# Four-layer network on one core: the join of the last two layers written in another order

## Chip, cores and metric

One Trainium2 chip, one of its cores. The metric is the device time of one execution in microseconds (us). Engines are named as in the profile: PE is TensorE, DVE is VectorE, ACT is ScalarE, POOL is GpSimd, SP is SyncE, whose queue here only issues transfers.

## What is computed

Four layers in a row, each `x = x + ffn(cond(x))`, on 4 sequences of 256 tokens with 256 features. The condition of a layer is a gain per token and feature (it depends on `side` and `cond`, not on x) times `sigmoid(x)`. The change lies between the last step of the third layer's feed-forward part and the first attention head of the fourth layer:

```python
# third layer, behind gate and up: RMS norm, a quantisation, the down product
h = rms_norm(h, ln_weight)
return bit_linear(h, w_down)          # rounds h per token to 8 bits, times ternary weights
...
# fourth layer
x = x + ao                            # ao: attention of 16 heads, each of 128
h = rmsnorm(x, ln1_w)
q = (h @ wq).reshape(b, s, H, HD)
k = (h @ wk).reshape(b, s, H, HD)
v = (h @ wv).reshape(b, s, H, HD)
scores = jnp.einsum('bqhd,bkhd->bhqk', q, k) / np.sqrt(HD)
attn = jax.nn.softmax(jnp.where(causal, scores, -1e9), axis=-1)
```

## The kernel before, in words

Every engine has its own list of instructions, written out by hand, and the lists meet at semaphores. T is 1,024 tokens, P is 128, W is 512; features lie on the partitions, in KD = 2 blocks, so that x consists of NCH = 4 chunks of 128 x 512. ORDER takes the two chunks of the first 512 tokens (n = 0, 1) ahead of those of the last 512 (n = 2, 3). A float32 product is made of three passes: a value is split in a high part (rounded to fp32r) and a low part (the rest), and the passes are high x high, low x high, high x low.

**The tail of layer 2 (the third layer).** The last four of eight tiles of 128 tokens, u = 4 to 7, go through this chain: `rounds(u)` on VectorE (L1551 H, then L1555 HQ, both 128x1024), `turn_hidden(u)` on TensorE (eight transposes, L1630), `product_turned(u)` on ScalarE (HT, L1461), `product(u)` on TensorE (L1641), `out(u)` on ScalarE (OT, L1468), `back(u)` on TensorE (two transposes, L1649). Behind back(7) lies the result of the last 512 tokens, which `residual(2)` and `residual(3)` (L2369) add to x.

**The head of layer 3 (the fourth layer).** For each half n of the tokens: `sigmoid` on ScalarE (L293), `with_gain` on VectorE (four pieces of 128x256 a half, L324, which give XC), then the norm: `squares` on ScalarE (L1709), `add_up` on TensorE (sums over the features, L1717), `means` on VectorE (L1724), `roots` on ScalarE (L1730, Sqrt), `factors` on VectorE (L1735), `spread_out` on TensorE (the factors to all partitions, L1741), `normalise` on VectorE (HN, L1750), `high` on ScalarE (XH, L1759), `low` on VectorE (XL, L1766).

**The weights.** A group g of two heads has 2,048 columns in RAW, four parts of 512 (GCOL). ScalarE makes the high part WH of each (L2244), GpSimd the low part WL (L2211, `split_low`). Group 0 is split by GpSimd in one go ahead of everything else of layer 3. The transfer of group 1 is issued when all four chunks of XC are there.

**Attention in halves.** `project(i, c)` makes one of six blocks of q, k and v of half i (c = 0, 1, 4, 5: six passes of 128x512, L2566; c = 2, 3: twelve of 128x256, L2561), into bank c % 2, which ScalarE (even c) or VectorE (odd c) empties (L2251, L2363). Half 0 is group 0 with the first 512 tokens, half 1 group 0 with the last 512. The steps of a half stand in a table, PLANS: S is scores (TensorE L2637, L2638; the row maximum on VectorE L2449; the exponential on ScalarE L2302), N divides by the sum (VectorE L2457, L2462), T turns (TensorE L2645, ScalarE L2309), A is attention times V (TensorE L2655, L2656), O the output product, D c the block c of the next half's projection, H a part of a later group's weights (ScalarE, then GpSimd). B occurs in PLANS[0] alone: spread_out, normalise, high and low of the second half of the tokens. All engines walk the same table, each doing its own share of a step. Before the first projection of a half 0 or 1 TensorE waits for the XL of its tokens:

```python
if c == 0 and half == 0:

    pe.wait_ge(w_low, 4 * g + 3)
if c == 0 and i < 2:

    pe.wait_ge(norm.xl, 2 * (i + 1))
```

Below stand the functions that the diff touches.

Of the kernel before, what the change touches and what calls it, by code (L numbers as in the profile page):

```python
# [1781 lines left out]
PLANS = {0: "S0 S1 B0 N0 H0 S2 H1 T0 N1 S3 D0 H2 T1 N2 D1 N3 D2 A0 T2 A1 T3 D3 A2 D4 A3 D5 H3".split(),  # L1782
# [30 lines left out]
def all_steps():  # L1813

    return [("C", n, 0) for n in range(6)] + [step for i in range(NHALF) for step in steps_of(i)]
# [264 lines left out]
def layer3(nc, k, io, ahead):  # L2080
# [3 lines left out]
    with ExitStack() as ctx:  # L2084
# [122 lines left out]
        def split_low(pool, g, m):  # L2207

            pool.wait_ge(w_high, 4 * g + m + 1)
            c = slice(m * GCOL, (m + 1) * GCOL)  # L2210
            pool.tensor_tensor(WL[g % 2][:, c], RAW[g % 2][:, c], WH[g % 2][:, c].bitcast(F32),  # L2211
                               ALU.subtract).then_inc(w_low, 1)

        @block.gpsimd
        def _(pool):
            ahead_gpsimd(pool)
            for m in range(4):
                split_low(pool, 0, m)

            pool.wait_ge(cond.xc, 2)  # L2220
            pool.memset(MASK[:], 0.0).then_inc(mask, 1)
            pool.wait_ge(mask, 1)

            pool.affine_select(out=MASK[:], in_=MASK[:], compare_op=ALU.is_ge, fill=NEG,
                               base=P, pattern=[[-1, 2 * P]], channel_multiplier=1).then_inc(mask, 1)
            for kind, n, at in all_steps():
                if kind == "H":
                    split_low(pool, at, n)
                    if (n, at) == (0, 1):
                        pool.memset(ex.TW[:, 0], 1.0).then_inc(ex.tw_one, 1)  # L2230
                if kind == "E":
                    ex.split_low(pool, at, n)
            ex.gpsimd(pool)
# [13 lines left out]
        def _(act):  # L2247

            def evacuated(i, c):
                if c % 2 == 0:  # L2250
                    evacuate(act, i, c, lambda out, in_: act.activation(out, in_, ACT.Copy))  # L2251
# [17 lines left out]
            product_turned(5)  # L2269
            out(4)  # L2270
            act.wait_ge(cond.xc, 2)
            norm.squares(act, 0)
            product_turned(6)
            out(5)
            product_turned(7)
            out(6)
            norm.roots(act, 0)
            out(7)
            norm.high(act, 0)
# [8 lines left out]
            evacuated(0, 4)  # L2288
            for kind, n, at in all_steps()[6:]:
# [33 lines left out]
                if kind == "B":  # L2323
                    norm.high(act, 1)
# [33 lines left out]
        def _(v):  # L2358
# [12 lines left out]
            def with_gain(n):  # L2371
                v.wait_ge(cond.sig, n + 1)
                v.wait_ge(k.g_done, LAYERS * NCH)
                conditioned(v, k, cond, 1, n)
# [4 lines left out]
            rounds(5)  # L2379
            with_gain(0)  # L2380
            with_gain(1)
            rounds(6)
            rounds(7)
            norm.means(v, 0)
            norm.factors(v, 0)
            v.wait_ge(ln_in, 16)
            norm.normalise(v, 0)
            norm.low(v, 0)
            residual(2)
            residual(3)  # L2390
            evacuated(0, 1)
            with_gain(2)
            with_gain(3)
            evacuated(0, 3)
            norm.means(v, 1)
            norm.factors(v, 1)
            evacuated(0, 5)
# [40 lines left out]
            for kind, n, at in all_steps()[6:]:  # L2438
# [38 lines left out]
                if kind == "B":  # L2477
                    norm.normalise(v, 1)
                    norm.low(v, 1)
# [43 lines left out]
        def _(pe):  # L2523
# [79 lines left out]
            turn_hidden(4)  # L2603
            turn_hidden(5)
            product(4)
# [3 lines left out]
            norm.add_up(pe, 0)  # L2609
# [5 lines left out]
            norm.spread_out(pe, 0)  # L2615
# [4 lines left out]
            for c in range(4, 6):  # L2620
                project(0, c)
            for kind, n, at in all_steps()[6:]:
# [40 lines left out]
                if kind == "B":  # L2663
                    norm.spread_out(pe, 1)
# [130 lines left out]
```

## Time and profile before

| | |
|---|---|
| median of 3 runs | 899.87 us (897.52, 899.87, 900.35) |
| profiled execution, its own time | 899.28 us |
| its span, first to last instruction | 897.6 us |
| TensorE busy (matmul) | 759.3 us, 85% |
| VectorE busy | 577.1 us, 64% |
| ScalarE busy | 437.8 us, 49% |
| GpSimd busy | 240.5 us, 27% |
| mean granted clock of TensorE | 0.931 |

The span is the time between the first and the last instruction; the execution's own time is 1.7 us longer. Busy shares are averages over four layers with different limits, so they do not tell what a change at one place is worth. The join lies between about 337 and 396 us of the span. The granted clock is a share of full speed: 1.00 is 2.4 GHz, 0.50 is 1.2 GHz. In the timeline a row gives the start, the duration, the engine, the line and the operation; in square brackets stands how long the engine had been idle before it and who released it. Where several like instructions are merged, the duration is that of all of them.

### The profile page before, as it was taken

What the parts mean: (1) busy time and instruction counts of PE and PEld (TensorE: products, weight loads), DVE (VectorE), ACT (ScalarE), POOL (GpSimd) and SP (SyncE); (2) the same over time, 40 slices, a digit from 0 to 9 for tenths busy, and PEclk for the clock granted to TensorE, in tenths of its full rate; (3) what the DMA queues carried; (4) which work ended last, traced back from release to release, by engine and by line L of the source; (5) the groups of instructions that cost most, each with busy time, mean ns of one, the idle gap of its engine ahead of it and who ended that gap; (6) DMA issues with size and microseconds to landing.
All of it is one profiled execution on the core that took longest, in us unless ns stands there. A gap on an engine that the chain in (4) does not pass through costs nothing.

```text
span 897.6 us, 11277 instructions
## 1 busy us (share of the span) xinstructions
PE 759.3 (85%) x3633; PEld 576.1 (64%) x3633; DVE 577.1 (64%) x1285; ACT 437.8 (49%) x878; POOL 240.5 (27%) x245
## 2 busy tenths in 40 slices
PE   1886785978785555799999999999969999999997
PEld 0433453634453134688888988888857888888885
DVE  5998889879988896556566566755664233232233
ACT  5895452235414646456455555654654334334342
POOL 5310112320140623011021021201111455555553
PEclk9999897789896878899999999999997999999998
DMA  4000003923222000210110101101010632323421
GB/s 149 2 1 1 0 0 111 381 66 106 82 71 70 1 0 1 94 48 1 48 39 11 47 1 48 37 1 37 1 38 11 154 95 59 95 46 73 93 55 47
DMA packets 37422, 49.84 MB, mean 56 GB/s; under 512 B 18574, under 2 KB 29942, under 8 KB 35702
## 3 DMA queue, kind: packets, MB, share of 16 engines
q1 hardware_dynamic: 36310, 46.90, 17.1%
q0 software_dynamic: 768, 2.10, 0.7%
q8 instruction: 30, 0.49, 0.2%
q10 hardware_dynamic: 288, 0.14, 0.1%
q14 instruction: 26, 0.21, 0.1%
HBM read 42.99 MB, written 6.13 MB: 55 GB/s over the span
## 4 chain that ended last, share of the span: by engine, by line
PE 59%; DVE 7%; ACT 2%; issue 1%; POOL 1%; DVEq 0%; ACTq 0%
PE bank L2000 15%; PE bank L2566 10%; PE bank L2016 8%; PE bank L2580 5%; PE bank L2561 5%; PE bank L2655 3%; PE bank L2638 3%; PE bank L2645 2%; PE bank L2656 2%; PE bank L2637 1%; PE bank L1614 1%; PE bank L1717 1%; DVE H L1551 1%; DVE XC L324 1%; DVE H L1530 1%
## 5 line engine op out<-in xcount | busy, mean ns | idle before, releaser
L2044 DVE TENSOR_TENSOR B_l<-bank,TW_l 128x512 f32<-128x512 f32 (+1 forms) x50 | 34.5, 691 | 134.3 <-PE bank L2000 131.3
L2211 POOL TENSOR_TENSOR WL<-RAW,WH 128x512 fp32r<-128x512 f32 x32 | 41.8, 1312 | 232.4 <-ACT WH L2244 232.4
L2069 POOL TENSOR_TENSOR HL_l<-H_l,HH_l 128x512 fp32r<-128x512 f32 (+1 forms) x50 | 64.9, 1298 | 121.9 <-ACT HH_l L2061 121.9
L2302 ACT ACTIVATE EX<-EX,nm 128x128 f32<-128x128 f32 (+1 forms) x128 | 57.0, 446 | 72.6 <-DVE nm L2453 72.6
L2053 ACT ACTIVATE S_l<-bank 128x512 f32<-128x512 f32 (+1 forms) x50 | 29.9, 599 | 86.1 <-PE bank L2000 85.9
L159 POOL TENSOR_TENSOR WV<-EUK,V 128x512 f32<-128x512 f32 x16 | 23.8, 1495 | 152.6 <-DVE GAIN L274 89.9
L2467 DVE TENSOR_TENSOR AL<-bank,AH 128x256 fp32r<-128x256 f32 x64 | 27.2, 424 | 56.6 <-ACT AH L2316 56.6
L2566 PE MATMUL bank<-XH,WH 128*128 128x512 f32 x128 | 60.3, 471 | 3.7 <-DVE XL L1766 2.8
L2000 PE MATMUL bank<-XH,WH 128*128 128x512 f32 (+1 forms) x136 | 55.0, 405 | 0.0
L2000 PE MATMUL bank<-XL,WH 128*128 128x512 f32 (+1 forms) x136 | 54.5, 401 | 0.0
L2000 PE MATMUL bank<-XH,WL 128*128 128x512 f32 (+1 forms) x136 | 54.5, 401 | 0.0
L2566 PE MATMUL bank<-XH,WL 128*128 128x512 f32 x128 | 51.9, 406 | 0.0
L2566 PE MATMUL bank<-XL,WH 128*128 128x512 f32 x128 | 51.7, 404 | 0.0
L2061 ACT ACTIVATE HH_l<-H_l 128x512 fp32r<-128x512 f32 (+1 forms) x50 | 31.5, 631 | 36.5 <-PE bank L2016 29.7
L2449 DVE CUSTOM_DVE_ANT_0 EX<-bank,MASK 128x128 f32<-128x128 f32 (+1 forms) x128 | 40.7, 355 | 13.1 <-PE bank L2638 12.5
L1983 POOL TENSOR_TENSOR WL<-RAW,WH 128x512 fp32r<-128x512 f32 x27 | 35.0, 1296 | 44.9 <-ACT WH L1976 44.9
L506 ACT ACTIVATE MARK<-SC,THR 128x1536 bf16<-128x1536 bf16 (+1 forms) x30 | 43.0, 1509 | 6.2 <-PE bank L727 6.2
L2462 DVE TENSOR_SCALAR PN<-EX,rr 128x128 f32<-128x128 f32 (+1 forms) x128 | 38.9, 353 | 2.5 <-PE bank L2645 0.2
L2655 PE MATMUL bank<-PT,V 128*128 128x256 f32 x128 | 38.4, 381 | 2.4 <-ACT PT L2309 2.4
L2638 PE MATMUL bank<-K,Q 128*128 128x256 f32 x128 | 38.7, 384 | 0.0
L2561 PE MATMUL bank<-WH,XH 128*128 128x256 f32 x128 | 38.5, 301 | 0.0
L2316 ACT ACTIVATE AH<-bank 128x256 fp32r<-128x256 f32 x64 | 24.6, 384 | 27.7 <-PE bank L2656 26.2
(319 smaller groups left out, 2198.5 us busy)
## 6 DMA issues: line engine op xcount, KB each, us to landing
RAW<-l_attn SPq DMA_DIRECT2D x8, 1024.0 KB, 4.8
WE<-l_experts SPq DMA_DIRECT2D x1, 6144.0 KB, 22.8
TW_l<-routed SPq DMA_DIRECT2D x14, 256.0 KB, 4.2
RAW<-l_w SPq DMA_DIRECT2D x3, 1024.0 KB
RAW<-l_experts SPq DMA_DIRECT2D x6, 512.0 KB, 3.9
TW_l<-routed SPq DMA_DIRECT2D x14, 192.0 KB, 3.3
sorted_x<-ZERO SPq DMA_DIRECT2D x1, 1920.0 KB, 8.0
XIN<-sorted_x SPq DMA_DIRECT2D x15, 128.0 KB, 2.2
```

Of the source, the lines that this page charges most:

```text
L506: act.activation(MARK[:, n % RING, 0:cols], SC[:, at:at + cols], ACT.Sign, bias=THR[:, i:i + 1]).then_inc(mark, 1)
L2000: mm = pe.matmul(self.k.banks[2 * ((q + 1) % 2) + o][0:rows], w[i % self.SLOTS][:, at:at + rows], x[:, h, n * W:(n + 1) * W], start=(s == ...
L2016: mm = pe.matmul(self.k.banks[4 + 2 * m + n][:], w[i % self.SLOTS][0:rows, at:at + P], x[0:rows, q % 4], start=((i, f, s) == (0, 0, 0)), s ...
L2069: pool.tensor_tensor(self.HL[0:rows, q % 4], self.H[0:rows, q % 2], self.HH[0:rows, q % 4].bitcast(F32), ALU.subtract).then_inc(self.h_low, 1)
L2211: pool.tensor_tensor(WL[g % 2][:, c], RAW[g % 2][:, c], WH[g % 2][:, c].bitcast(F32), ALU.subtract).then_inc(w_low, 1)
L2302: act.activation(EX[:, s, a:b], EX[:, s, a:b], ACT.Exp, bias=nm[:, s, i:i + 1], scale=scale, accum_out=rs[:, s, i:i + 1]).then_inc(expd, 1)
L2449: v.tensor_tensor_reduce(EX[:, s, a:b], banks[2 + s][:, a:b], MASK[:, 2 * P - (b - a):], 1.0, NEG, ALU.add, ALU.max, accum_out=mx[:, s, i: ...
L2561: mm = pe.matmul(out[:, a * 2 * HD:(a + 1) * 2 * HD], x[:, h, t * P:(t + 1) * P], w[slot][:, at:at + 2 * HD], start=(p == 0), stop=(p == l ...
L2566: mm = pe.matmul(out[:], w[slot][:, at:at + HD], x[:, h, half * W:(half + 1) * W], start=(p == 0), stop=(p == len(passes) - 1))
L2580: mm = pe.matmul(banks[m][:], w[g % 2][:, at:at + P], x[:, head, here(i)], start=(head == 0 and p == 0), stop=(head == 1 and p == 2))
L2638: pe.matmul(out[:, P:3 * P], Q[:, n // 2, c + P:c + SEQ], K[:, n // 2, c:c + SEQ], start=True, stop=True).then_inc(scores, 1)
L2655: pe.matmul(out[:, 0:SEQ], V[:, t, d], PT[:, s, 0:SEQ], start=True, stop=False)
```

## The change

Four things are written in another order; no arithmetic is added or taken away.

- `split_low` of group 0: GpSimd's four instructions become four of VectorE, put between its other steps. GpSimd waits for them (`w_low` at 4) before it goes on with the later groups.
- The first half's norm moves ahead in the tail of layer 2: with_gain(0) and (1) stand ahead of rounds(5), means and factors ahead of rounds(7), add_up behind product(4), spread_out behind turn_hidden(5).
- "Conditions other half ahead of first keys": with_gain(2) and (3) stand ahead of the evacuation of the first key block, `evacuated(0, 1)`.
- The second half's factors go between projections: spread_out(1) between project(0, 4) and project(0, 5), normalise and high right behind; low becomes the step K0 at the head of PLANS[0], B0 is gone, and in the table the first projections of half 1 (D0, D1) stand ahead.

```diff
-PLANS = {0: "S0 S1 B0 N0 H0 S2 H1 T0 N1 S3 D0 H2 T1 N2 D1 N3 D2 A0 T2 A1 T3 D3 A2 D4 A3 D5 H3".split(),
+PLANS = {0: "K0 S0 S1 D0 H0 N0 S2 H1 T0 N1 D1 T1 S3 N2 D2 A0 H2 T2 N3 D3 A1 T3 A2 D4 A3 D5 H3".split(),
...
         @block.gpsimd
         def _(pool):
             ahead_gpsimd(pool)
-            for m in range(4):
-                split_low(pool, 0, m)
...
+            pool.wait_ge(w_low, 4)
             for kind, n, at in all_steps():
...
         @block.scalar
...
             product_turned(4)
-            product_turned(5)
-            out(4)
             act.wait_ge(cond.xc, 2)
             norm.squares(act, 0)
+            out(4)
+            norm.roots(act, 0)
+            product_turned(5)
             product_turned(6)
             out(5)
+            norm.high(act, 0)
             product_turned(7)
             out(6)
-            norm.roots(act, 0)
             out(7)
-            norm.high(act, 0)
...
             norm.roots(act, 1)
             evacuated(0, 4)
+            norm.high(act, 1)
...
-                if kind == "B":
-                    norm.high(act, 1)
...
         @block.vector
...
             residual(0)
             residual(1)
             rounds(4)
-            rounds(5)
+            split_low(v, 0, 0)
             with_gain(0)
             with_gain(1)
+            rounds(5)
             rounds(6)
+            norm.means(v, 0)
+            split_low(v, 0, 1)
+            norm.factors(v, 0)
             rounds(7)
-            norm.means(v, 0)
-            norm.factors(v, 0)
             v.wait_ge(ln_in, 16)
             norm.normalise(v, 0)
+            split_low(v, 0, 2)
             norm.low(v, 0)
+            split_low(v, 0, 3)
             residual(2)
             residual(3)
-            evacuated(0, 1)
             with_gain(2)
             with_gain(3)
+            evacuated(0, 1)
             evacuated(0, 3)
             norm.means(v, 1)
             norm.factors(v, 1)
+            norm.normalise(v, 1)
             evacuated(0, 5)
...
-                if kind == "B":
-                    norm.normalise(v, 1)
+                if kind == "K" and at == 0:
                     norm.low(v, 1)
...
         @block.tensor
...
             turn_hidden(4)
+            product(4)
+            norm.add_up(pe, 0)
             turn_hidden(5)
-            product(4)
+            norm.spread_out(pe, 0)
             turn_hidden(6)
             product(5)
             back(4)
-            norm.add_up(pe, 0)
             turn_hidden(7)
             product(6)
             back(5)
             product(7)
             back(6)
-            norm.spread_out(pe, 0)
             back(7)
             for c in range(4):
                 project(0, c)
             norm.add_up(pe, 1)
-            for c in range(4, 6):
-                project(0, c)
+            project(0, 4)
+            norm.spread_out(pe, 1)
+            project(0, 5)
...
-                if kind == "B":
-                    norm.spread_out(pe, 1)
```

TensorE in the tail of layer 2, before, from the sums of the first half (L1717) to the spreading of its factors (L1741); L1630 are transposes of HQ, L1641 products, L1649 transposes back:

```order
L1717 MATMUL bank4<-ONES,SQ3 128x1 x8
L1630 MATMUL bank1<-IDB,HQ2 128x128 x8
L1641 MATMUL bank2<-WT2,HT2 128x256 x8
L1649 MATMUL bank5<-IDF,OT2 128x128
L1649 MATMUL bank7<-IDF,OT2 128x128
L1641 MATMUL bank3<-WT2,HT2 128x256 x8
L1649 MATMUL bank5<-IDF,OT2 128x128
L1649 MATMUL bank7<-IDF,OT2 128x128
L1741 MATMUL bank6<-IDF,rstd3 128x128 x4
```

The same place in the change, from product(4) on:

```order
L1641 MATMUL bank2<-WT2,HT2 128x256 x8
L1717 MATMUL bank4<-ONES,SQ3 128x1 x8
L1630 MATMUL bank1<-IDB,HQ2 128x128 x8
L1741 MATMUL bank6<-IDF,rstd3 128x128 x4
L1630 MATMUL bank0<-IDB,HQ2 128x128 x8
L1641 MATMUL bank3<-WT2,HT2 128x256 x8
L1649 MATMUL bank5<-IDF,OT2 128x128
```

The sums now stand behind the first of four products, and the factors behind one set of transposes more; three products and three sets of transposes back, which stood ahead of the factors, now stand behind them.

VectorE from the first half's means (L1724) on, before:

```order
L1724 TENSOR_SCALAR ms3<-bank4 128x4
L1735 RECIPROCAL rstd3<-rt3 128x4
L1750 SCALAR_TENSOR_TENSOR HN3<-XC,LN3,bank6 128x512 x2
L1766 TENSOR_TENSOR XL3<-HN3,XH3 128x512 x2
L2369 TENSOR_TENSOR X<-X,bank5 128x512
L2369 TENSOR_TENSOR X<-X,bank7 128x512
L2363 COPY K3<-bank1 128x512
```

and in the change, where L2211 is `split_low`, L1551 and L1555 are rounds(7), and L2368 is the residual:

```order
L1724 TENSOR_SCALAR ms3<-bank4 128x4
L2211 TENSOR_TENSOR WL3_0<-RAW3_0,WH3_0 128x512
L1735 RECIPROCAL rstd3<-rt3 128x4
L1551 TENSOR_SCALAR H2<-H2,s2_2 128x1024
L1555 TENSOR_SCALAR HQ2<-H2 128x1024
L1750 SCALAR_TENSOR_TENSOR HN3<-XC,LN3,bank6 128x512 x2
L2211 TENSOR_TENSOR WL3_0<-RAW3_0,WH3_0 128x512
L1766 TENSOR_TENSOR XL3<-HN3,XH3 128x512 x2
L2211 TENSOR_TENSOR WL3_0<-RAW3_0,WH3_0 128x512
L2368 TENSOR_TENSOR X<-X,bank5 128x512
```

Three of the four low parts of the weights stand between the steps of the norm, and rounds(7) stands behind the factors (L1735) where it stood ahead of the means.

TensorE at the start of PLANS[0], before: scores of steps 0 and 1, the second half's factors (L1741), scores of step 2, the first turn (L2645), scores of step 3, then the first projection of half 1 (L2566):

```order
L2637 MATMUL bank2<-K3,Q3 128x128
L2638 MATMUL bank2<-K3,Q3 128x256
L2637 MATMUL bank3<-K3,Q3 128x128
L2638 MATMUL bank3<-K3,Q3 128x256
L1741 MATMUL bank7<-IDF,rstd3 128x128 x4
L2637 MATMUL bank2<-K3,Q3 128x128
L2638 MATMUL bank2<-K3,Q3 128x256
L2645 MATMUL bank4<-IDF,PN3 128x128 x3
L2637 MATMUL bank3<-K3,Q3 128x128
L2638 MATMUL bank3<-K3,Q3 128x256
L2566 MATMUL bank0<-XH3,WH3_0 128x512
```

and in the change (its line numbers are 3 or 4 higher), from the end of the first scores on:

```order
L2642 MATMUL bank2<-K3,Q3 128x256
L2641 MATMUL bank3<-K3,Q3 128x128
L2642 MATMUL bank3<-K3,Q3 128x256
L2569 MATMUL bank0<-XH3,WH3_0 128x512
L2569 MATMUL bank0<-XL3,WH3_0 128x512
L2569 MATMUL bank0<-XH3,WL3_0 128x512
L2569 MATMUL bank0<-XH3,WH3_0 128x512
L2569 MATMUL bank0<-XL3,WH3_0 128x512
L2569 MATMUL bank0<-XH3,WL3_0 128x512
L2641 MATMUL bank2<-K3,Q3 128x128
L2642 MATMUL bank2<-K3,Q3 128x256
L2649 MATMUL bank4<-IDF,PN3 128x128 x3
```

The first projection of half 1 (six passes) stands ahead of the scores of step 2 and of the first turn, and the factors are no longer in between.

## Rows read from the trace of the kernel before

**Rows 1.** The page, first part: busy us, share of the span and count by engine

```profile
PE 759.3 (85%) x3633; PEld 576.1 (64%) x3633; DVE 577.1 (64%) x1285; ACT 437.8 (49%) x878; POOL 240.5 (27%) x245
```

**Rows 2.** By stretch: length, busy PE, PEld, DVE, ACT, POOL, clock, DMA share, GB/s

```profile
357.00:358.00 1.00, 0.00 (x0) 0.00 (x0) 0.96 (x2) 0.97 (x2) 0.00 (x0) 0.94 0.00 0
...
395.70:651.00 255.30, 254.39 (x1497) 224.46 (x1496) 162.07 (x590) 141.06 (x416) 35.68 (x28) 1.00 0.09 28
```

**Rows 3.** The chain that ended last, in order of time: start, us, what

```profile
359.02 5.47 PE bank L2566 x12
...
382.70 2.56 PE bank L2566 x6
385.26 0.35 PE bank L2645 x3
385.61 1.39 PE bank L2566 x6
```

**Rows 4.** Timeline of TensorE: start, us, engine, line, operation, idle before and releaser

```profile
342.31 1.04 PE L1630 MATMUL bank<-IDB,HQ 128*128 128x128 bf16 x8 [4.88 <-DVE HQ L1555]
...
345.54 1.92 PE L1641 MATMUL bank<-WT,HT 128*128 128x256 bf16 x8
...
349.30 1.84 PE L1717 MATMUL bank<-ONES,SQ 128*128 128x1 f32 x16
...
352.73 1.05 PE L1641 MATMUL bank<-WT,HT 128*128 128x256 bf16 x8
...
354.82 1.16 PE L1741 MATMUL bank<-IDF,rstd 128*128 128x128 f32 x8 [0.82 <-DVE rstd L1735]
...
359.02 0.77 PE L2566 MATMUL bank<-XH,WH 128*128 128x512 f32 x1 [2.83 <-DVE XL L1766]
...
368.03 1.95 PE L1717 MATMUL bank<-ONES,SQ 128*128 128x1 f32 x16 [0.66 <-ACT SQ L1709]
...
380.52 0.90 PE L2645 MATMUL bank<-IDF,PN 128*128 128x128 f32 x3 [4.82 <-DVE PN L2462]
```

**Rows 5.** Timeline of VectorE

```profile
338.74 1.84 DVE L1551 TENSOR_SCALAR H<-H,s 128x1024 f32<-128x1024 f32 x1
...
344.57 1.66 DVE L324 SCALAR_TENSOR_TENSOR XC<-SG_l,GF,GAIN 128x256 f32<-128x256 f32 x4
346.15 0.75 DVE L1551 TENSOR_SCALAR H<-H,s 128x1024 f32<-128x1024 f32 x1
...
354.59 0.18 DVE L1735 RECIPROCAL rstd<-rt 128x4 f32<-128x4 f32 x1 [3.25 <-ACT rt L1730]
...
357.53 1.35 DVE L1766 TENSOR_TENSOR XL<-HN,XH 128x512 fp32r<-128x512 f32 x2
...
378.35 2.12 DVE L2462 TENSOR_SCALAR PN<-EX,rr 128x128 f32<-128x128 f32 x2
...
381.56 0.55 DVE L2462 TENSOR_SCALAR PN<-EX,rr 128x128 f32<-128x128 f32 x2
```

**Rows 6.** Timeline of GpSimd

```profile
337.53 5.85 POOL L2211 TENSOR_TENSOR WL<-RAW,WH 128x512 fp32r<-128x512 f32 x4 [7.71 <-ACT WH L2244]
...
378.04 1.32 POOL L2211 TENSOR_TENSOR WL<-RAW,WH 128x512 fp32r<-128x512 f32 x1 [30.09 <-ACT WH L2244]
```

**Rows 7.** Timeline of ScalarE

```profile
340.32 1.15 ACT L293 ACTIVATE SG_l<-X 128x512 f32<-128x512 f32 x2
...
351.65 1.02 ACT L1461 ACTIVATE HT<-bank 128x1024 bf16<-128x1024 bf16 x1 [1.37 <-PE bank L1630]
...
353.06 1.28 ACT L1730 ACT_TABLE_LOAD   x1
354.35 0.20 ACT L1730 ACTIVATE rt<-ms 128x4 f32<-128x4 f32 x1
...
356.87 1.29 ACT L1759 ACTIVATE XH<-HN 128x512 fp32r<-128x512 f32 x2 [1.95 <-DVE HN L1750]
```

**Rows 8.** Transfers into the tile RAW, 366 to 380 us: time from issue to landing

```profile
DMA to landing us min/median/max: 4.7/6.4/8.0
```

More of the change, by code:

```diff
@@ L2205, in _, with split_low @@
             sp.wait_ge(stored, 16 * NCH)
-        def split_low(pool, g, m):
-            pool.wait_ge(w_high, 4 * g + m + 1)
+        def split_low(eng, g, m):
+            eng.wait_ge(w_high, 4 * g + m + 1)
             c = slice(m * GCOL, (m + 1) * GCOL)
-            pool.tensor_tensor(WL[g % 2][:, c], RAW[g % 2][:, c], WH[g % 2][:, c].bitcast(F32),
+            eng.tensor_tensor(WL[g % 2][:, c], RAW[g % 2][:, c], WH[g % 2][:, c].bitcast(F32),
                                ALU.subtract).then_inc(w_low, 1)
```

## Prediction

> **What bounds the kernel now.** I read the page first: TensorE is busy 85% of the span, every other engine much less [rows 1]. That average says nothing about the join, so I took busy time by stretch. From 395.7 to 651 us TensorE works 254.39 of 255.30 us at a granted clock of 1.00 (2.4 GHz) [rows 2]: once attention is in its stride TensorE alone sets the end, and every microsecond by which half 1 begins earlier reaches the end of the program. Half 1 begins at 395.7. Then I read the timelines of the four engines between 337 and 396 us for what TensorE waits for:
>
> - 4.88 us ahead of the transposes at 342.31, until VectorE has written HQ [rows 4];
> - 2.83 us ahead of the first projection at 359.02, until XL is there [rows 4];
> - 0.66 us ahead of the second half's sums at 368.03, for the squares [rows 4];
> - 4.82 us ahead of the first turn at 380.52, for PN [rows 4].
>
> Two waits cost more than their length. In the stretch from 357 to 358 us the granted clock leaves 1.00, with TensorE without work [rows 2], and the twelve matmuls of the first two projections then take 5.47 us; six take 1.39 us at full clock [rows 3]. The same shows behind the wait for PN: 2.56 us for six at 382.70, against 1.39 for the next six [rows 3].
>
> **The change part by part.** I followed each engine's new list by hand with the durations of the rows.
>
> *VectorE up to the gains.* GpSimd's four low parts lie from 337.53 to 343.4 [rows 6], and beside them an H of 1,024 columns takes 1.84 us, where it takes 0.75 alone [rows 5]. The change takes GpSimd's work away from here. H and HQ of tile 4 then take about 1.4 us (338.74 to 340.15) and one low part on VectorE 0.63: it has shape and types of XL, whose pair takes 1.35, and starts are 0.63 apart [rows 5]. That is a near match, so its bounds are close: 0.6 to 0.7. The first sigmoid is ready at about 340.9 [rows 7], and the four pieces of gain take 1.6 us [rows 5]: XC is there at 342.5 instead of 346.2.
>
> *The factors.* The transposes of tile 4 start at 340.2 instead of 342.31, HT at 341.5 behind the sigmoids, product(4) at 342.4 with 1.92 us as at half clock [rows 4]. ScalarE makes the squares meanwhile. The sums take 1.8 us [rows 4] behind product(4), to 346.0. Mean 0.17, root 0.2, one low part 0.63 and reciprocal 0.18: factors at 346.9 instead of 354.8 [rows 5]. The Sqrt table load of 1.28 us [rows 7] falls between 344.6 and 345.9, while TensorE adds up, and costs nothing; were the sums 1.3 us faster it would be what is waited for.
>
> *Start of the projections.* The factors are spread by 348.2. HN takes 1.4 to 349.7, then come a low part, XH of two chunks (1.29 us for the pair [rows 7]) and XL by 352.0. TensorE is not ready for it: behind the spreading stand two sets of transposes, three products (0.87 us to the next start at full clock, 1.05 each in the row [rows 4]) and the transposes back. HT of tile 7 waits on ScalarE behind the two XH until 351.2 and takes 0.95 to its end [rows 7], product(7) 352.2, OT 0.42, and the last transposes end at 353.8. The first projection starts there: **5.2 us earlier** than 359.02. What is late next is thus the tail of layer 2, not the norm; XL, and with it the three low parts put ahead, has 1.8 us in hand.
>
> *Clock at the first projections.* Ahead of it TensorE now has gaps of 0.9 and 0.3 us where it had 0.82 and 2.83. Two projections at full clock take 2.8 instead of 5.47 [rows 3]: **2.6 us**. Bounds: 0 if the clock is at 1.2 GHz again, 2.7 if not.
>
> *Conditions ahead of the first keys.* Between 353.9 and 357.0 VectorE does residual(2), (3) and the gains, the squares are ready at 358.2, and the sums of the second half are due behind projection 3 at 359.3. The wait goes: **0.7 us** [rows 4]. The key block is emptied at 357.6 and its bank is wanted at 358.0; if the cover of 0.3 us is gone, it costs what the gains are late. The transfer of group 1's weights is issued with the gains, at 357 instead of 367, lands at most 8.0 us later [rows 8], at 365, and ScalarE wants it at 369.9: nothing.
>
> *Factors between the projections, and the plan.* Spreading (0.9 us) only changes place. The new wait there would be for the reciprocal: sums end at 361.0, the root is at 361.5, projection 4 covers until 362.4. After projection 5 (364.7) VectorE empties a bank and makes XL (1.9 us) while TensorE does two scores (1.3): a wait of 0.7 for half 1's first projection. Then the row maxima (0.8), the exponential (0.9) and N (0.75) against projection 6 and the scores (2.0): a wait of 0.5 at the first turn. The old wait of 4.8 us had room for HN, XL and N in a row; now HN is made under projection 5. And GpSimd's low parts of group 1 now run beside N of steps 1 to 3. One such meeting stands in the rows: a pair of PN takes 2.12 us beside a low part of 1.32, and 0.55 without [rows 5, 6]. Following the starts, two of the three meet it for a part, 0.7 to 0.8 us at TensorE. Sum: 4.8 - 0.7 - 0.5 - 0.8 = **2.8 us**. Bounds: 4.8 if nothing is waited for, 0 if the chain is as long as before.
>
> *Clock behind it.* At 380.52 the turn takes 0.90 against 0.35, the projection 2.56 against 1.39, and the scores between them 0.9 against 0.65 [rows 3, 4]: **2.0 us**, all of which hangs on there being no wait of several microseconds.
>
> *Nothing* for GpSimd (it waits for work there), for SP and for the new wait of GpSimd for the four low parts, done at 352.6, 18 us ahead of its next.
>
> Sum: 5.2 + 2.6 + 0.7 + 2.8 + 2.0 = 13.3. The profiled execution took 899.28 us, so 886.0; the median of the runs is 0.6 above it: **886.6 us**.
>
> *Two rules weighed.* The table load takes 1.28 us and the activation behind it starts 0.01 us after its end [rows 7]. The Trainium skill ("ScalarE: Activation LUTs", What ACT_TABLE_LOAD costs) adds a drain of about 1.38 us to each switch. By that rule the root and all behind it would come 1.1 us later and the sum would be 12.2 instead of 13.3; the row is of the same instruction, so I keep 13.3.
>
> The meeting of PN with a low part costs between 0.7 and 0.8 us by the starts [rows 5, 6]. The Trainium skill ("SBUF — State Buffer", Who interferes with whom) says that the one of VectorE and GpSimd that comes second is held for the whole of the other's instruction. By that rule, if all three meetings fell worst, the loss would be three times 1.3 us instead of 0.8, and the sum 10.2; the trace agrees that the loser waits (1.57 us lost in the pair above) but the starts that I follow are not the worst.
>
> **The rivals.**
>
> *A: low clock at the first projections.* The gaps of 0.9 and 0.3 us and a partly idle stretch before 346 suffice to keep or bring 1.2 GHz. For it: it fell after a wait of 2.83 us only [rows 2, 4]. Against it: until 354 it stood with gaps of like size. Time: 886.6 + 2.6 = 889.2.
>
> *B: the stall at the first turn comes back.* The exponential needs its table (1.28) behind XH, N needs VectorE behind XL and the maxima, and GpSimd holds PN. If that is as long as before, 2.8 and 2.0 us are not gained: 891.4.
>
> *C, slower than before: TensorE stays at 1.2 GHz through the whole stretch.* The change replaces long waits by short ones; if these keep the clock low from 341 until half 1 begins, the first two projections cost 2.6 us more, the ten others 2.56 - 1.39 = 1.17 each, so 11.7, and turns, scores and products with V some 3.5 (0.9 of it stands in the term for the clock above). Time: 886.6 + 17.8 = 904.4, slower by 0.5%. It decides from 13.3 us on, about ten projections at half clock. Against it: in this trace continuous projections brought the clock back each time, after the 5.47 us for twelve matmuls and ahead of the 1.39 at 385.61 [rows 3], and the stretch is mostly such work.
>
> *D: no change.* The trace has no other limit ahead of 395.7 that could swallow 13 us, and the listing shows the steps moved as described, so this is left with the smallest chance.
>
> **How the numbers follow.** Forecast 0.66, A 0.16, B 0.12, C 0.02, D 0.02, and 0.02 for A and B together (894). The range: below, all new waits (2.0 us) vanish and the run lies 1.1 low, as 897.52 to 900.35 scatter by 1.4 about their middle: 883.5. Above it takes in A and B: 891.5. About 0.3% (2.7 us) is what a measurement of this kernel can tell from no change. Faster by more than that, under 897.2: forecast, A, B and both, 0.96; within: 0.02; slower: 0.02.
>
> **What would show it.** Right: no GpSimd work from 330 to about 370 us except the mask; H near 0.78 us each; factors near 347; the first projection at 353 to 355 behind the last transposes back, not behind XL; its two first blocks in 2.8 us; no wait over 1 us at the first turn; half 1 at 381 to 383; from there to the end the same length as before. Wrong: a first projection released by XL, a wait for PN over 2 us, six matmuls of 2.5 us behind 354, or a tail from half 1 on that is longer than 502 us.

## The result, and the profile after

The changed kernel takes 887.58 us (median of 4 runs, 886.44 to 892.8) against 899.99 us before: a ratio of 0.9877, 95% interval 0.9853 to 0.9902. Forecast were 886.6 us and a range of 883.5 to 891.5. The profiled execution took 887.66 us with a span of 885.9; before, 899.28 and 897.6. So the size came out within 1 us, but the two largest of the five terms of the sum behind it did not, and part of the agreement is luck; the section on the prediction says which part.

The page, first part, of the changed kernel, as [rows 1]:

```profile
span 885.9 us, 11278 instructions
PE 758.4 (86%) x3633; PEld 573.6 (65%) x3633; DVE 576.8 (65%) x1289; ACT 437.6 (49%) x878; POOL 234.4 (26%) x241
```

TensorE runs the same number of instructions, and its busy time over the whole program is the same to 0.9 us. The join, the stretch in which the change acts, tells more: TensorE is busy there for 42.6 of 58.2 us before and for 40.5 of 49.0 now, so 7.0 of the 9.1 us that went are waiting and 2.1 are busy time, which hangs on the clock. Timeline of TensorE in the tail of layer 2 and at the first projections (as [rows 4]):

```profile
341.06 0.62 PE L1630 MATMUL bank<-IDB,HQ 128*128 128x128 bf16 x8 [2.84 <-DVE HQ L1555]
343.23 1.89 PE L1641 MATMUL bank<-WT,HT 128*128 128x256 bf16 x8 [1.54 <-ACT HT L1461]
344.91 3.41 PE L1717 MATMUL bank<-ONES,SQ 128*128 128x1 f32 x16
349.26 2.07 PE L1741 MATMUL bank<-IDF,rstd 128*128 128x128 f32 x8
...
355.59 1.05 PE L1641 MATMUL bank<-WT,HT 128*128 128x256 bf16 x8 [0.80 <-ACT HT L1461]
...
357.20 0.44 PE L1649 MATMUL bank<-IDF,OT 128*128 128x128 f32 x2 [0.35 <-ACT OT L1468]
357.39 0.48 PE L2569 MATMUL bank<-XH,WH 128*128 128x512 f32 x1
```

The first projection now starts right behind the last transposes back, as forecast, and not behind XL. It starts at 357.39, not at 353.8. The sums (L1717) take 3.41 us (1.84 before) and the spreading (L1741) 2.07 (1.16 before). Busy time by stretch says why; the columns are those of [rows 2], and the second fence is the kernel before:

```profile
341.00:342.00 1.00, 0.62 (x8) 0.45 (x8) 0.83 (x3) 0.99 (x3) 0.00 (x0) 0.88 0.00 0
...
350.00:351.00 1.00, 1.00 (x7) 1.00 (x6) 0.57 (x1) 0.26 (x1) 0.00 (x0) 0.50 0.00 0
352.00:353.00 1.00, 1.00 (x12) 0.92 (x11) 1.00 (x3) 0.81 (x1) 0.00 (x0) 1.00 0.00 0
```

```profile
346.00:347.00 1.00, 1.00 (x6) 0.73 (x5) 0.97 (x3) 0.81 (x1) 0.71 (x1) 0.50 0.00 0
...
349.00:350.00 1.00, 1.00 (x12) 1.00 (x10) 0.22 (x1) 1.00 (x3) 0.00 (x0) 1.00 0.00 0
```

The granted clock is 0.50 from 341.75 to 352.0 us. It fell behind TensorE's idle stretch up to 341.06; in the kernel before it fell within the idle stretch up to 342.31 and stood at 0.50 from 340.8 to 347.6. So two things differ: sums and spreading, which used to come after the clock had risen, now come before that, and the stretch at half clock is 10.2 us long instead of 6.8. VectorE shows the rest (as [rows 5]):

```profile
339.53 0.75 DVE L1551 TENSOR_SCALAR H<-H,s 128x1024 f32<-128x1024 f32 x1
340.31 0.69 DVE L1555 TENSOR_SCALAR HQ<-H 128x1024 bf16<-128x1024 f32 x1
340.92 0.68 DVE L2211 TENSOR_TENSOR WL<-RAW,WH 128x512 fp32r<-128x512 f32 x1
341.78 1.67 DVE L324 SCALAR_TENSOR_TENSOR XC<-SG_l,GF,GAIN 128x256 f32<-128x256 f32 x4 [0.17 <-ACT SG_l L293]
...
349.04 0.17 DVE L1735 RECIPROCAL rstd<-rt 128x4 f32<-128x4 f32 x1
...
372.59 0.55 DVE L2466 TENSOR_SCALAR PN<-EX,rr 128x128 f32<-128x128 f32 x2
...
374.23 2.47 DVE L2466 TENSOR_SCALAR PN<-EX,rr 128x128 f32<-128x128 f32 x2
```

H takes 0.75 instead of 1.84 us, a low part 0.68, and the gains stand at 343.36. All lies 0.8 us later than in the profile before, because the first residual already did (338.33 against 337.53), ahead of everything that was changed. The last row is GpSimd's doing; its timeline, as [rows 6]:

```profile
374.38 1.28 POOL L2211 TENSOR_TENSOR WL<-RAW,WH 128x512 fp32r<-128x512 f32 x1 [29.23 <-ACT WH L2244]
375.61 0.95 POOL L2230 MEMSET TW_l<- 128x1024 f32 x1
376.51 1.31 POOL L2211 TENSOR_TENSOR WL<-RAW,WH 128x512 fp32r<-128x512 f32 x1
```

The second PN of the pair ends only when the low part and the memset behind it are both done. TensorE's waits in the stretch from 325 to 400 us: in total, times, longest:

```profile
PE bank L1630 <- DVE HQ L1555: 5.8, 3, 2.8
PE bank L1641 <- ACT HT L1461: 3.4, 3, 1.5
PE bank L2649 <- DVE PN L2466: 2.4, 3, 1.6
PE bank L1641 <- DVE OT L1560: 0.7, 1, 0.7
PE bank L1649 <- ACT OT L1468: 0.7, 2, 0.3
PE bank L2569 <- DVE XL L1766: 0.7, 1, 0.7
```

The wait of 4.82 us for PN has become three waits of 2.4 together. The one of 2.83 for XL ahead of the first projection and the one for the squares are gone; the 0.7 for XL is a new wait, ahead of half 1's first projection.

**Where the 11.7 us of span are.** I cut each profile at three points: the first residual of layer 3, the first projection, and the first scores of half 1. The join is what lies between the first and the last of these.

| us | before | changed | changed, second profile |
|---|---|---|---|
| first residual at | 337.53 | 338.33 | 336.85 |
| from there to the first projection | 21.49 | 19.06 | 18.94 |
| first projection to half 1 | 36.67 | 29.97 | 29.06 |
| join | 58.16 | 49.03 | 48.00 |
| half 1 to the end | 501.9 | 498.5 | 501.9 |
| span | 897.6 | 885.9 | 886.8 |

The join gave 9.1 us where 13.3 were forecast. In the first profile 3.4 us came from the end of attention, where nothing was changed. Busy time by stretch there, first before, then changed:

```profile
675.00:680.00 5.00, 5.00 (x22) 4.56 (x20) 0.00 (x0) 0.00 (x0) 0.00 (x0) 0.53 0.01 3
680.00:685.00 5.00, 5.00 (x14) 3.94 (x14) 0.34 (x2) 1.49 (x2) 0.00 (x0) 0.50 0.00 0
```

```profile
666.00:671.00 5.00, 4.65 (x23) 4.13 (x23) 0.00 (x0) 0.16 (x1) 0.20 (x1) 0.66 0.02 7
671.00:676.00 5.00, 5.00 (x27) 4.27 (x27) 2.15 (x5) 2.42 (x4) 0.00 (x0) 1.00 0.00 0
```

At the same place of the program the clock stood at 0.50 for 10.2 us in one and for 3.4 in the other. These 3.4 us of span are therefore no gain of the change.

### The profile page after: what moved, and what is told of

Read it like the earlier page. It is cut to its first block, busy times and chain, and to the rows that moved or that the text cites. A ratio compares the mean times of both kernels' runs of the same rounds, so it can differ in the third digit from the quotient of the medians.

```text
span 885.9 us, 11278 instructions
## 1 busy us (share of the span) xinstructions
PE 758.4 (86%) x3633; PEld 573.6 (65%) x3633; DVE 576.8 (65%) x1289; ACT 437.6 (49%) x878; POOL 234.4 (26%) x241
## 4 chain that ended last, share of the span: by engine, by line
PE 58%; DVE 6%; ACT 3%; issue 1%; POOL 1%; DVEq 0%; ACTq 0%
PE bank L2000 15%; PE bank L2569 10%; PE bank L2016 8%; PE bank L2583 5%; PE bank L2564 5%; PE bank L2659 3%; PE bank L2642 3%; PE bank L2649 2%; PE bank L2660 1%; PE bank L2641 1%; PE bank L1614 1%; PE bank L1717 1%; DVE PN L2466 1%; PE bank L1641 1%; DVE H L1530 1%
## 5 line engine op out<-in xcount | busy, mean ns | idle before, releaser
L2211 POOL TENSOR_TENSOR WL<-RAW,WH 128x512 fp32r<-128x512 f32 x28 | 35.9, 1284 | 219.2 <-ACT WH L2244 219.2
L1983 POOL TENSOR_TENSOR WL<-RAW,WH 128x512 fp32r<-128x512 f32 x27 | 35.0, 1295 | 44.9 <-ACT WH L1976 44.9
```

## The experiments

The kernels were measured in three groups, and those of one group share their runs of the kernel before: median 898.49 us (18 runs) for the first four below, 899.04 (11 runs) for factors behind, old table and all together, 898.9 (11 runs) for the others. The ratios are to these. "Changed" is the changed kernel.

### The changed kernel again

Nothing is edited.

> The changed kernel unaltered, for the size and for its place. In its first profile the join (start of the first residual of the last layer to the first scores of half 1) was 9.0 us shorter than before (49.2 for 58.2), yet the span was 11.7 us shorter; 3.4 us of the rest lie at the first experts, where the clock was at 1.2 GHz for 3.4 us instead of 10.2. Theory (that part is how the execution happened to fall): the profile here has a half-clock stretch at the experts of some other length, and the times scatter between 9 and 13 us below before, ratio about 0.988. Rival (the change makes it shorter there too): the stretch is again 3.4 us long and the ratio stays at 0.987 or below.

Measured: 888.11 us, ratio 0.988 (0.9859 to 0.9902). The profile has 10.2 us at half clock at the experts and takes 501.9 us from half 1 to the end, as before. The theory holds: the 3.4 us of the first profile were how that execution fell (one of the six runs, 892.24 us, lies outside the expected scatter). By the medians the gain is 10.4 us here, close to the 10.2 of this profile's join. The join is 48.0 here, 1.0 shorter: the waits for PN sum to 1.5 instead of 2.4.

```profile
PE bank L2649 <- DVE PN L2466: 1.5, 3, 0.7
```

### The low parts back on GpSimd

```diff
             ahead_gpsimd(pool)
+            for m in range(4):
+                split_low(pool, 0, m)
...
             rounds(4)
-            split_low(v, 0, 0)
             with_gain(0)
...
             norm.means(v, 0)
-            split_low(v, 0, 1)
...
             norm.normalise(v, 0)
-            split_low(v, 0, 2)
             norm.low(v, 0)
-            split_low(v, 0, 3)
```

> The changed kernel with group 0's four low parts back on GpSimd. Theory (they hold VectorE up): H and HQ of tile 4 take 3.4 instead of 1.4 us, the gains are ready about 2 us later, and so is the first projection, 21 us behind the first residual instead of 19.1; time 1.5 to 2.5 us above the changed kernel. Rival (the cost of a low part is VectorE's own 0.6 us, wherever it stands): the factors come 0.6 us earlier, and the time is the same or up to 0.6 us lower.

Measured: 893.25 us, ratio 0.9931 (0.9911 to 0.9951), 5.1 above changed in the same group. VectorE's timeline:

```profile
339.46 1.84 DVE L1551 TENSOR_SCALAR H<-H,s 128x1024 f32<-128x1024 f32 x1
341.33 1.64 DVE L1555 TENSOR_SCALAR HQ<-H 128x1024 bf16<-128x1024 f32 x1
342.90 2.67 DVE L324 SCALAR_TENSOR_TENSOR XC<-SG_l,GF,GAIN 128x256 f32<-128x256 f32 x4
```

and GpSimd's in the same kernel:

```profile
338.25 5.84 POOL L2211 TENSOR_TENSOR WL<-RAW,WH 128x512 fp32r<-128x512 f32 x4 [7.72 <-ACT WH L2246]
```

The first projection comes 21.63 us behind the first residual. That is the 21.49 of before: **without the move of the low parts the rest of the new tail order gains nothing up to the first projection.** The theory holds up to the first projection, with a size somewhat above its 21 us: the gains are held too (2.67 instead of 1.67 us), and the low clock lasts 13.7 us instead of 10.2. The time is another matter: 5.1 us where 1.5 to 2.5 were expected. The join (51.57) is 2.5 us longer than in the first profile of changed, which has the same waits for PN (2.4), and 3.6 longer than in the second. The rest lies outside the join, where the two kernels are the same, and is not explained. The low parts alone, moved in the old tail order, were not run, so what they are worth without the new order is open.

### The tail alone, and the plan alone

Tail alone is changed with the second half's norm, the keys and the table as before; plan alone is the kernel before with these three as in the change. Below is tail alone against changed, with cuts marked; plan alone against the kernel before is the same diff read the other way.

```diff
 tail alone, against changed
-PLANS = {0: "K0 S0 S1 D0 H0 N0 S2 ...
+PLANS = {0: "S0 S1 B0 N0 H0 S2 H1 ...
...
-            project(0, 4)
-            norm.spread_out(pe, 1)
-            project(0, 5)
+            for c in range(4, 6):
+                project(0, c)
...
+            evacuated(0, 1)
             with_gain(2)
             with_gain(3)
-            evacuated(0, 1)
```

> The changed tail of layer 2 and the splits on VectorE alone; keys ahead of the gains, B0 and the old table. Theory (the parts act apart): first projection 19.1 us behind the first residual (before 21.5), its first twelve matmuls at full clock (2.8 for 5.5 us), the wait of 0.7 for the squares and the wait of 4.8 for PN with half clock behind it as before; join 53.1 us, time 5.1 us below before, 894.9. Rival (the stall behind the projections belongs to the tail): with projections at full clock the wait for PN gets longer and eats the 2.7 us; time 897 to 898.

> The old tail with splits on GpSimd, but gains ahead of keys, factors between the projections and the new table. Theory (the parts act apart): first projection 21.5 us behind the first residual and the first twelve matmuls at half clock, 5.5 us; no wait for the squares, waits in half 0 of some 2 to 3 us instead of 4.8, full clock from there: join 53 to 54 us, time 4 to 5 us below before, about 895.5. Rival (the clock was low because of the stall ahead, and stays low): one more stretch of 3 to 7 us at 1.2 GHz in half 0, time 897 to 899.

| us | time | ratio (95%) | to first projection | from there to half 1 | join |
|---|---|---|---|---|---|
| tail alone | 895.27 | 0.9967 (0.9955 to 0.998) | 18.95 | 35.75 | 54.70 |
| plan alone | 896.04 | 0.9965 (0.9951 to 0.9979) | 21.49 | 32.56 | 54.05 |
| changed | 888.11 | 0.988 (0.9859 to 0.9902) | 18.94 | 29.06 | 48.00 |

The tail brings the forecast start, and the wait for PN is there as before:

```profile
361.49 2.18 PE L1717 MATMUL bank<-ONES,SQ 128*128 128x1 f32 x16 [0.69 <-ACT SQ L1709]
375.58 0.90 PE L2649 MATMUL bank<-IDF,PN 128*128 128x128 f32 x3 [4.83 <-DVE PN L2466]
```

From the first projection on it gains 0.9 us where 2.7 were expected. The wait for PN did not grow (4.83 us), so the rival is not the reason: the clock, full at first, fell for 3.4 us at 363.1, in the sums behind the wait of 0.69, which costs half its length, 1.7 us; it fell again, for 6.8 us, in the wait for PN, as in the kernel before. Plan alone has the join that the theory gave it, 54.05 us, half clock at the first projections and full clock from there on. The parts gain 3.5 and 4.1 us of join, 7.6 in sum, and both together 9.1 and 10.2 in the two profiles. Of the difference, the 1.7 us of clock at 363.1 are seen: in tail alone part of what the projections gained by full clock was lost again behind the wait for the squares, which the plan takes away. By the medians the parts gained less than expected, 3.2 us (5.1) and 2.4 us (4 to 5).

### Keys ahead of the gains

```diff
+            evacuated(0, 1)
             with_gain(2)
             with_gain(3)
-            evacuated(0, 1)
             evacuated(0, 3)
```

> The changed kernel with the first keys emptied ahead of the gains of the other half again. Theory: the squares are ready some 1.6 us later, TensorE waits 0.6 to 0.7 us ahead of the second half's sums, as before the change; join 0.7 us longer. Rival (a later wait, for XL ahead of half 1's first projection, takes it up): the same join. By the times not to be told apart; the profile decides.

Measured: 892.24 us, ratio 0.9921 (0.9895 to 0.9947), join 50.70. The wait is back, with its length as expected:

```profile
362.94 2.14 PE L1717 MATMUL bank<-ONES,SQ 128*128 128x1 f32 x16 [0.78 <-ACT SQ L1709]
```

but the join is 2.7 us longer than in the second profile of changed, which has the same waits for PN (1.5), and not 0.7. Behind the wait the clock is at 1.2 GHz for 3.4 us from 364.5 on:

```profile
365.00:366.00 1.00, 1.00 (x4) 0.81 (x4) 0.34 (x2) 0.20 (x1) 0.00 (x0) 0.50 1.13 475
```

Neither profile of changed has this, nor has any other of the kernels without the wait. One instruction's place on VectorE thus costs 0.8 us of wait and about 1.7 of clock. The size expected was too small. The time is 4.1 us above that of changed, which was measured in another group; the intervals of the two ratios just touch.

### Factors behind the sixth projection; the old table

```diff
             project(0, 4)
-            norm.spread_out(pe, 1)
             project(0, 5)
+            norm.spread_out(pe, 1)
...
-            norm.normalise(v, 1)
             evacuated(0, 5)
+            norm.normalise(v, 1)
```

> The changed kernel with the second half's spreading behind the sixth projection instead of ahead of it (and HN behind the last evacuation). Theory (HN under the sixth projection is what shortens the chain to XL): half 1's first projection waits 2.2 us instead of 0.7, join 1.5 us longer, and 1.7 more if the clock falls by it. Rival (the new table alone hides it): wait under 1 us, the same join.

Measured: 891.53 us, ratio 0.9894 (0.9868 to 0.9921); the wait for XL is 1.6 us where 2.2 were expected, the join 49.83. That is 0.8 us more than the profile of changed with the same waits for PN (2.4). Half the expected size, in its direction; the clock did not fall there. The runs lie in two clusters, 886.4 and 887.1, and four from 891.5 to 892.2, so the median says little about 0.8 us.

```diff
-PLANS = {0: "K0 S0 S1 D0 H0 N0 S2 H1 T0 N1 D1 T1 S3 N2 D2 A0 H2 T2 N3 D3 A1 T3 A2 D4 A3 D5 H3".split(),
+PLANS = {0: "K0 S0 S1 N0 H0 S2 H1 T0 N1 S3 D0 H2 T1 N2 D1 N3 D2 A0 T2 A1 T3 D3 A2 D4 A3 D5 H3".split(),
```

> The changed kernel with the old table in the old order, but for B0, which stays split into the factors between the projections and K0. Theory (both are needed: the factors early take 1.7 us off the old wait of 4.8, the projections moved ahead cover the rest): the first turn waits 2.6 us, the waits for XL and at the second turn go; join 0 to 1 us longer, and 1.7 to 2 us more if the clock falls. Rival (the factors between the projections did all of it): join the same or shorter, no half clock.

Measured: 890.94 us, ratio 0.9912 (0.9893 to 0.993); join 50.28, 1.3 to 2.3 us longer than changed. The waits are not the one of 2.6 that was expected. TensorE's in this kernel, same stretch:

```profile
PE bank L2649 <- DVE PN L2466: 1.6, 2, 1.0
PE bank L2564 <- ACT Q L2251: 1.4, 1, 1.4
PE bank L2641 <- DVE mx L2453: 1.3, 1, 1.3
```

The clock stays full through all of them. The first two in time, 1.3 for mx and 1.0 for the first PN, stand on one chain, from HN, XL and the row maxima on VectorE over the exponential to PN; together they are 2.3 us, close to the 2.6 that the theory had, in two places instead of one. The other two, 0.6 for the second PN and the 1.4 for Q, stand behind VectorE's nm of 128 x 2 values, which takes 0.17 us elsewhere. The chain of waits shows nm, and GpSimd's timeline in the same kernel shows what runs beside it:

```profile
372.96 1.25 DVE nm L2457
...
376.14 1.02 DVE nm L2457
```

```profile
372.91 1.28 POOL L2211 TENSOR_TENSOR WL<-RAW,WH 128x512 fp32r<-128x512 f32 x1 [28.71 <-ACT WH L2244]
...
375.83 1.29 POOL L2211 TENSOR_TENSOR WL<-RAW,WH 128x512 fp32r<-128x512 f32 x1 [0.73 <-ACT WH L2244]
```

Each nm ends 0.02 to 0.04 us behind the low part. So the table is needed beside the early factors, as the theory said; about half of what the old table waits for is the chain that it named, and the other half is VectorE held by GpSimd, which it did not name.

### The memset behind the low parts

```diff
-                    if (n, at) == (0, 1):
+                    if (n, at) == (3, 1):
                         pool.memset(ex.TW[:, 0], 1.0).then_inc(ex.tw_one, 1)
```

> The changed kernel with GpSimd's memset of TW behind the fourth low part of group 1 instead of the first. Theory (N of step 1 was held by a low part and the memset behind it: 2.47 us for the pair, 1.64 us of wait at the second turn, 0.7 in the second profile): the pair takes at most 1.9 us, the wait at the second turn is under 0.8, the join 0.3 to 0.9 us shorter; by the times not to be told from the changed kernel. Rival (the low part alone holds it): second low part then starts right behind the first and holds the pair as long; no difference.

Measured: 888.94 us, ratio 0.9881 (0.9856 to 0.9906), waits for PN 1.5 us, join 48.22. The same waits as in the second profile of changed, where the memset stood in its old place: there VectorE got in ahead of it (a pair of PN 1.58 us), in the first profile it did not (2.47). The profiles of all experiments say more than this one. With the new table and the memset early, the pair takes 2.46 to 2.48 us in five and 1.58 in three; with the memset late it takes 1.58 and 1.59 in both kernels that have it so. So the memset is what the 0.9 us are, when it comes in between; two profiles are too few to say that the worse case is gone. By the times it is nothing.

### TensorE kept at work, in the tail and at the experts

```diff
+            def fill(bank, n):
+                for _ in range(n):
+                    pe.transpose(banks[bank][:, 0:P], k.IDF[:], k.IDF[:])
+
+            fill(5, 22)
             turn_hidden(4)
+            fill(5, 12)
             product(4)
             norm.add_up(pe, 0)
...
+            for _ in range(28):
+                pe.transpose(banks[4][:, 0:P], k.IDF[:], k.IDF[:])
             ex.down_pair(pe, 0)
```

The two places were tried alone and then together with the late memset.

> The changed kernel with TensorE kept at work in its two waits of the tail: 22 transposes of the identity into a free bank ahead of turn_hidden(4), 12 ahead of product(4). In both profiles of the changed kernel the clock went to 1.2 GHz for 10.2 us there, and the sums took 3.4 us and the spreading 2.1, where the prediction had 1.8 and 1.2. Theory (the missing 2.8 us ahead of the first projection are the clock): the clock stays at 1.00, sums 1.7, spreading 1.1, first projection 16.3 to 16.8 us behind the first residual instead of 19.0; time 2.3 to 2.7 us below the changed kernel. Rival (HT and OT on ScalarE or HQ on VectorE bound the tail): the clock is full but the first projection stays at 18.5 to 19; the same time.

TensorE's timeline in the first of them:

```profile
338.17 2.56 PE L2608 MATMUL bank<-IDF 128*128 128x128 f32 x22
...
344.80 1.95 PE L1717 MATMUL bank<-ONES,SQ 128*128 128x1 f32 x16 [0.41 <-ACT SQ L1709]
...
347.69 1.16 PE L1741 MATMUL bank<-IDF,rstd 128*128 128x128 f32 x8 [0.47 <-DVE rstd L1735]
...
349.50 1.91 PE L1641 MATMUL bank<-WT,HT 128*128 128x256 bf16 x8
```

The sums take 1.95 and the spreading 1.16 us again, and the first projection comes 17.30 us behind the first residual instead of 19.0. So 1.7 of the missing 2.8 us were the clock. It still fell once, for 3.4 us at 348.7 (a product takes 1.91). A half of these 3.4 us is 1.7, more than the 1.0 that is still missing, so the clock can account for all of it, and nothing is left for the rival. The time is 888.53 us, ratio 0.988 (0.9854 to 0.9905), where 2.3 to 2.7 us below changed were expected: the 1.7 us of the profile do not show in it, and with runs from 887.93 to 890.17 nothing more can be said.

> The changed kernel with 28 transposes of the identity in TensorE's wait of 3.9 us for the first hidden low part, where attention ends and the experts begin. Four profiles have 10.2 us at 1.2 GHz there, one (the first of the changed kernel) 3.4, and from half 1 to the end they take 501.9 and 498.5 us. Theory (that wait alone makes the clock fall): full clock, 496.5 to 497.5 us from half 1 to the end, median 4 to 5 us below the changed kernel. Rival (the clock falls by an earlier, thinner stretch): 10.2 or 3.4 us at 1.2 GHz as before, times the same.

Measured: 885.01 us, ratio 0.9832 (0.9802 to 0.9863), 496.8 us from half 1 to the end as the theory had it, full clock there:

```profile
661.66 3.22 PE L2682 MATMUL bank<-IDF 128*128 128x128 f32 x28
665.74 0.47 PE L2016 MATMUL bank<-HH_l,WH 128*128 128x512 f32 x1 [0.86 <-POOL HL_l L2069]
```

So filling the wait of 3.9 us, which leaves 0.9, keeps the clock up there, and the fall had cost 5.1 us (half of 10.2). This also fits the 3.4 us of the first profile, which are half of the 6.8 us of half clock by which it was shorter. By the medians the gain on changed is 3.1 us where 4 to 5 were expected; the join of this profile (48.99) is 1.0 us longer than in the second of changed.

> The changed kernel with the transposes of e7 and of e8 and the memset of e6. Theory (each clock gain is independent): first projection 17.3 us behind the first residual, join 46.4, 496.8 us from half 1 to the end, span about 881.5, median about 883, 16 us below before. Rival (a gain at one place is given back at another, as the times of e7 did not go down with its join): no better than e8, 885.

Measured: 882.88 us (882.0 to 883.99), ratio 0.9821 (0.98 to 0.9841), join 46.59, 498.4 us from half 1 to the end (one stretch of 3.4 us at half clock, at 646.3, ahead of the filled wait). The gain is near the theory's. It is below the kernel with the tail's waits filled (888.53); from the one with the experts' wait filled (885.01) it cannot be told apart, as the intervals of the ratios overlap, so the rival is not ruled out. Part of the agreement is luck: the span of 880.9 holds a first residual at 335.94, 0.9 to 2.4 us earlier than in changed, ahead of all that was edited, which makes up for the 1.6 us by which the end is longer than expected.

## Why the prediction was right, and where it was not

*VectorE up to the gains.* Right to about 0.1 us: counted from the first residual, the gains are ready after 5.03 us, forecast were 5.0. The low part took 0.68 and H 0.75. The run with GpSimd's low parts shows that the earlier start is not had without this term.

*The factors and the start of the projections*, forecast 5.2 us earlier, measured 2.4 and 2.5. What is late next was named rightly (the tail of layer 2; the projection follows the transposes back), its size was wrong. The step that failed: "The sums take 1.8 us". That row was taken at full clock; product(4) just ahead had been priced at half clock, and the sums behind it should have been too. They took 3.3 us to the next start instead of 1.7, the spreading 1.9 instead of 1.0, and the products and transposes behind it came later. Nor was it foreseen that the clock would stay low for 10.2 us instead of 6.8. Keeping the clock up brought 1.7 of the 2.8 us back.

*Clock at the first projections*, 2.6 us: right. The 5.47 ran to the end of the last matmul and the 2.8 from start to start; start to start it is 5.26 against 2.85, and the block behind it gains 0.1 more.

*Conditions ahead of the first keys*, 0.7 us: the wait went, and in the kernel before no fall of the clock followed it, so the term is right as a part of the sum. Beside the other parts it is worth more: undoing it in changed cost 2.7 us, 0.8 of wait and 1.7 of clock, which the prediction did not have.

*Factors between the projections, and the plan*, 2.8 us, the second term that was too large. The wait for XL was 0.68 (0.7 forecast), at the first turn 0.26 (0.5). Meetings with GpSimd were priced at 0.8; at the second and the fourth turn they were 1.64 + 0.51 in one profile, 1.2 for both in the other. The part is then 1.7 to 2.6 us. The memset behind the low part was not in the sum at all, though it stands in the kernel before too:

```profile
379.31 0.95 POOL L2230 MEMSET TW_l<- 128x1024 f32 x1
```

The pair of PN there starts at 378.35 and ends at 380.47, 0.2 us behind the memset and 1.1 behind the low part. The prediction read its 1.57 us of loss as the low part's alone. The held instructions bear out the rule of the Trainium skill ("SBUF — State Buffer", Who interferes with whom) more than the 0.8 that the sum took: in the first profile of changed PN waits out a low part and a memset, 1.9 us lost.

*Clock behind it*, 2.0 us: right, no half clock between 352 us and half 1.

*The table load*: 1.28 us, ended at 346.9, ahead of the mean at 348.5, so neither of the prediction's two readings could show in the time of changed. The kernel with the tail's waits filled decides: its load ends at 346.41 and the root starts at 346.98, when the mean is there. That is 0.57 us behind the load, and there is no room for 1.38.

Together the join gave 9.1 and 10.2 of 13.3 us; the terms as measured add up to 9.4 and 10.4, and 0.2 to 0.3 us stay over. That the forecast of 886.6 and the measured 887.58 agree better than that is luck, since executions differ elsewhere: the first profile gained 3.4 us at the experts and lost 0.8 ahead of the join. The repeat, with more runs of both kernels, has a gain of 10.4 us where the forecast had 13.3. The ratio's interval at the top, 8.8 to 13.2 us below before, holds the join's 9 to 10; the forecast's own gain lies just outside it. Rival A did not come about at the projections but one step ahead of them; B came about in part (the wait for PN is half of what it was, without the clock); C and D did not.

## What to carry to other kernels

Moving a low-priority job off GpSimd can be worth more than its own time: in the new tail order with the low parts on GpSimd, VectorE's H, HQ and gains are held by 3.0 us together (1.09, 0.95 and 1.00), while the four low parts cost VectorE 0.68 us each. When a step is moved to another place, price it at the clock granted at the new place, and look for what TensorE did just ahead of it. And a wait of TensorE can have a second price behind it: here 3.9 us of wait cost 5.1 us more in the profile, and filling it with idle work was worth 3.1 us by the medians, against 10.4 for the whole reordering.

## What the runs showed that was not expected

- A wait of 0.7 or 0.8 us for the squares was followed by 3.4 us at 1.2 GHz in tail alone and in keys first. The kernel before has a wait of 0.66 at the same place, with the clock at 1.00 since 364.7, and its clock did not fall until 378.35; changed, with waits of 0.7 and 1.6 us a little later, and the old table, with up to 1.4, kept full speed too. What sets these apart was not settled.
- The sixteen small matmuls of the sums, with one column each, are no less bound to the clock than the large ones: 3.3 us to the next start at half clock, 1.7 at full.
- VectorE's nm, 128 x 2 values, took 1.25 us instead of 0.17 beside GpSimd (the kernel with the old table). A small instruction was held for 1.1 us, about as long as a large one.
- After the clock fell at the experts, TensorE was busy 5.00 of 5.00 us in two stretches in a row of the kernel before and still had half clock. It had it for 10.2 us in most profiles whose wait is not filled, and for 3.4, 6.8 and 13.7 in one each (changed, old table, factors behind). Why it differs was not settled.
